# A transformer block on one core: side products in pairs of 64-row tiles between longer bursts of scores

## The reference

```python
h = _layernorm(x) * (1 + ca) + sa
qkv = (h @ qkv_w.T).reshape(B, S, 3, H, hd)             # B=4, S=1024, H=16, hd=16
scores = einsum('bhqd,bhkd->bhqk', q, k) * scale
out = einsum('bhqk,bhkd->bhqd', softmax(scores), v)
x = x + ga * (out.reshape(B, S, D) @ proj_w.T + proj_b)
h = _layernorm(x) * (1 + cb) + sb
base = h @ W_base + b_base
hid = relu(einsum('btd,ndh->nbth', h, W_enc) + b_enc)   # 8 experts of 64
recon = einsum('nbth,nhd->nbtd', hid, W_dec) + b_dec
adp = connected_idx[argmin(mean((recon - h) ** 2))]     # one per batch
mid = relu(h @ W_down[adp] + b_down[adp])
x = x + gb * (base + mid @ W_up[adp] + b_up[adp])
```

## Time and profile before

| | |
|---|---|
| median of 3 runs | 971.86 us (970.64 to 972.51) |
| the profiled execution, its own time | 975.65 us |
| its span in the trace | 973.8 us |
| PE busy | 938.1 us (96% of the span), 5890 matmuls |
| PEld (weight loads) busy | 489.1 us (50%) |
| DVE busy | 792.8 us (81%) |
| ACT busy | 656.7 us (67%) |
| POOL busy | 373.6 us (38%) |
| chain that ended last, share of PE | 76% |

### The profile page before, as it was taken

How to read it: one execution, slowest core, us unless ns; L and a number is a source line. 1 busy time by engine, 2 the same in 40 slices (tenths; PEclk the granted TensorE clock), 3 DMA queues, 4 the chain that set the end, 5 groups by cost and what they waited for, 6 DMA issues and landing times.

```text
span 973.8 us, 16714 instructions
## 1 busy us (share of the span) xinstructions
PE 938.1 (96%) x5890; PEld 489.1 (50%) x5890; DVE 792.8 (81%) x1629; ACT 656.7 (67%) x1295; POOL 373.6 (38%) x497
## 2 busy tenths in 40 slices
PE   6899999999999999999999999999999899999997
PEld 4443344434444555555444555645445465644486
DVE  4799989999788888877897888876887778888365
ACT  2148888888588677666679677575777756667930
POOL 4050265225366354121746645121655312115320
PEclk9889999999899999999999999999999999999999
DMA  7832061253444210555150511526123500141101
GB/s 179 142 73 45 23 115 58 60 122 82 70 75 77 59 45 25 83 82 168 48 86 20 94 57 35 83 54 170 52 64 53 77 8 29 41 129 59 30 6 50
DMA packets 51427, 68.78 MB, mean 71 GB/s; under 512 B 12347, under 2 KB 35648, under 8 KB 51332
## 3 DMA queue, kind: packets, MB, share of 16 engines
q1 hardware_dynamic: 50108, 66.84, 32.1%
q0 software_dynamic: 384, 0.79, 0.6%
q10 hardware_dynamic: 852, 0.09, 0.1%
HBM read 29.31 MB, written 12.59 MB: 43 GB/s over the span
## 4 chain that ended last, share of the span: by engine, by line
PE 76%; DVE 10%; ACT 4%; DMA 3%; SPq 2%; issue 2%; POOL 1%; ACTq 0%; DVEq 0%
PE pE L849 26%; PE pM L849 21%; PE pO L849 20%; PE pX L849 7%; DVE mx L1344 6%; DMA QO<-lo 2%; ACT P L1170 2%; SPq L1949 1%; DMA xin<-in_x 1%; DVE junk L1538 1%; ACT h2l_full L1257 1%; SPq L2009 1%; DMA P<-in_wmod 0%; DVE junk L1481 0%; ACT h1l_full L1211 0%
## 5 line engine op out<-in xcount | busy, mean ns | idle before, releaser
L1344 DVE TENSOR_REDUCE mx<-pM 128x1 f32<-128x512 f32 x458 | 298.6, 682 | 43.7 <-PE pM L849 41.6
L1170 ACT ACTIVATE P<-pM 128x512 f32<-128x512 f32 x464 | 260.2, 602 | 70.7 <-PE pM L849 69.4
L1344 DVE TENSOR_REDUCE mx<-pE 128x1 f32<-128x512 f32 x428 | 284.2, 681 | 28.9 <-PE pE L849 27.8
L1170 ACT ACTIVATE P<-pE 128x512 f32<-128x512 f32 x413 | 240.5, 602 | 83.4 <-PE pE L849 82.7
L849 PE MATMUL pO<-P,V 128*17 128x512 f32 x2048 | 261.0, 604 | 0.3 <-ACT P L1170 0.2
L849 PE MATMUL pM<-KO,QO 48*128 48x512 f32 x458 | 182.7, 456 | 8.2 <-DMA QO<-lo 6.5
L849 PE MATMUL pE<-KO,QO 48*128 48x512 f32 x428 | 179.0, 445 | 2.1 <-DVE mx L1344 1.3
L849 PE MATMUL pM<-QO,KO 50*128 50x512 f32 x464 | 174.1, 435 | 0.9 <-DVE mx L1344 0.5
L849 PE MATMUL pE<-QO,KO 50*128 50x512 f32 x413 | 170.7, 440 | 1.5 <-DVE mx L1344 1.0
L849 PEld LDWEIGHTS pM<-QO,KO 50*128 50x128 f32 x464 | 80.6, 188 | 85.0 <-issue 58.3
L849 PEld LDWEIGHTS pE<-QO,KO 50*128 50x128 f32 x413 | 73.8, 187 | 98.0 <-issue 76.5
(11 more groups left out here) (351 smaller groups left out, 1395.8 us busy)
## 6 DMA issues: line engine op xcount, KB each, us to landing
outs<-osb SPq DMA_DIRECT2D x31, 256.0 KB, 2.1
KO<-hi SPq DMA_DIRECT2D x56, 128.0 KB, 4.0
QO<-hi SPq DMA_DIRECT2D x56, 128.0 KB, 5.8
x<-in_x SPq DMA_DIRECT2D x20, 256.0 KB, 3.4
out<-x SPq DMA_DIRECT2D x16, 256.0 KB, 2.1
AT<-outs SPq DMA_DIRECT2D x15, 256.0 KB
asum<-wsum SPq DMA_DIRECT2D x15, 256.0 KB
KO<-lo SPq DMA_DIRECT2D x28, 128.0 KB, 4.1
```

The lines of the kernel that those rows point to most:

```text
L1170: e.activation(P[:, u % 3, j, :], bank(s), ACT.Exp).then_inc(*empties(s))
L1344: e.tensor_reduce(mx[:, hq % 2, k:k + 1, kh], bank(s), AX.X, ALU.max, negate=True).then_inc(*empties(s))
```

## The change

The side steps of `mate` (`qk` and `v` of batches 1 to 3, `enc`, `half`, `gsq`, `base`, `out`, `proj`, apart from most of those behind the last E) come in pairs of two neighbouring steps. Each product is cut along its contraction in rows 0 to 63 and rows 64 to 127. The first step takes the lower rows while the second takes the upper ones, then they swap (`together`), so that a pair stands in the same 64-row form as the scores. A pair is cut in six chunks, three before and three after the swap; the fourth waits for the last matmul of the third (`s_swap`). In the main loop a pair gets a mixed burst of eight pairs of scores, with a chunk behind the second to the seventh (`MIXED`); both steps' banks stay held over it. A burst without a side pair is still of three. `long` is gone; pieces that don't pair are placed singly. The planner's lags and due times change with it. In the hand-written end, `gsq` of the last half moves ahead of the second pieces of three `half` steps, and DVE splits `wdn` into `wdh` and `wdl` one step earlier, with `mid` waiting for `wdl` only ahead of its third matmul.

```diff
-SHARE = (1.3, 1.8, 2.2, 2.4)
+SHARE = (1.0, 1.0, 0.8, 0.8)
+CAP = 3
+MIXED = (0, 1, 1, 1, 1, 1, 1, 0)
+def mate(s):
+    i = 2 if s[0] in ("half", "gsq", "v", "enc", "base", "proj", "out") else 3
+    if s[0] not in ("half", "gsq", "v", "enc", "base", "proj", "out", "qk") or s[i] % 2:
+        return None
+    if s[0] in ("qk", "v") and s[1] == 0 or s[0] in ("proj", "out") and s[1] == LAST and (s[0] == "out" or s[2] > 1):
+        return None
+    return s[:i] + (s[i] + 1,) + s[i + 1:]
...
-        for _ in range(BURST):
+        credit = min(credit + SHARE[min(int(u) // UB, LAST)], CAP)
+        both = next_of("pair", u) if credit >= 1 and m < NM - 9 and at + len(MIXED) <= 4 * pv + 12 else None
+        credit -= both is not None
+        parts_done = 0
+        for i in range(1, (len(MIXED) if both else BURST) + 1):
...
+            for _ in range(MIXED[i - 1] if both else 0):
+                chunk(both, u, parts_done)
+                parts_done += 1
...
+            def products(s, h):
+                kind, b, k = s[:3]
+                o, r = bank(s), slice(64 * h, 64 * h + 64)
...
+                    if kind == "out":
+                        m0, r_ = 128 * (tt % 4), slice(64, 65) if h else slice(0, 64)
+                        got.append((region, hidden_of(b, k // 2)[r_, m0:m0 + 128], wug[r_, :]))
+                return got
+            def together(first, second, q):
+                if q == 0:
+                    inputs(first)
+                    inputs(second)
+                p, i = divmod(q, 3)
+                if q == 3:
+                    pe.wait_ge(*swap.now())
+                both = list(zip(products(first, p), products(second, 1 - p)))
+                n = len(both)
+                for k in range(n * i // 3, n * (i + 1) // 3):
+                    x, y = both[k]
+                    a = mm(*x, start=p == 0 and k == 0, stop=p == 1 and k == n - 1)
+                    z = mm(*y, start=p == 0 and k == 0, stop=p == 1 and k == n - 1)
+                if q == 2:
+                    z.then_inc(*swap.up())
...
-    for i in range(2):
-        for p in range(3):
-            fill(first[1][p], i)
-    now(("gsq", q, 0, 1), ("gsq", q, 1, 1), first[1][3], ("pick", q))
+    for p in range(3):
+        fill(first[1][p], 0)
+    now(("gsq", q, 0, 1), ("gsq", q, 1, 1))
+    for p in range(3):
+        fill(first[1][p], 1)
+    now(first[1][3], ("pick", q))
...
-                elif s == ("mid", LAST, 0) and not piece:
+                elif s == ("base", LAST, 3) and not piece:
```

More of the change, by code:

```diff
@@ L272, in come, with can, chunk @@
         for s in due.get(u, ()):
-            queue = waiting["short" if s[0] in SHORT else "quiet" if s[0] in QUIET else "long"]
+            if s in seconds:
+                continue
+            seconds.add(mate(s))
+            queue = waiting["short" if s[0] in SHORT else "quiet" if s[0] in QUIET else "pair" if mate(s) else "long"]
             queue.insert(sum(w[0] == "qk" for w in queue) if s[0] == "qk" else len(queue), s)
+    def can(s, u):
+        return all(done.get(p, u + 1) + lag <= u for p, lag in before(s) + (before(mate(s)) if mate(s) else []))
+    def chunk(s, u, q):
+        out.extend([(s, q // 5), (mate(s), q // 5, s)] if q in (0, 5) else [("chunk", s, mate(s), q)])
+        if q == 5:
+            done[s] = done[mate(s)] = u
+            if s[0] == "qk":
+                moving.extend(copies(4 * s[1] + s[2]))
     def next_of(queue, u, two=False):
@@ L284, in next_of @@
                 continue
-            if all(done.get(p, u + 1) + lag <= u for p, lag in before(s)):
+            if can(s, u):
                 waiting[queue].remove(s)
-                return (s, 0) if s[0] in PIECES else s
+                return (s, 0) if s[0] in PIECES and queue != "pair" else s
         return None
-    def ready(u):
-        return len(begun) + sum(all(done.get(p, u + 1) + lag <= u for p, lag in before(s)) for s in waiting["long"])
     def put(s, u):
         out.append(s)
-        step, p = s if isinstance(s[0], tuple) else (s, 0)
+        step, p = s[:2] if isinstance(s[0], tuple) else (s, 0)
         if p + 1 < PIECES.get(step[0], 1):
@@ L345, in alone_long @@
                 put(s, u)
+                if begun:
+                    put(begun.pop(), u)
     def alone(u0):
         for i in range(2):
-            out.extend(("E", u0 + i, j) for j in range(4))
+            both = next_of("pair", u0 + i)
+            for j in range(4):
+                out.append(("E", u0 + i, j))
+                if both and j % 2:
+                    for q in range(3 * (j // 2), 3 * (j // 2) + 3):
+                        chunk(both, u0 + i, q)
             if i == 0:
@@ L375, in weigh, with beside @@
             waiting["quiet"][:0] = [("oput", hq)] + [(k, *part) for k in ("oget", "orec", "osum", "onorm") if last]
-    credit, at, pv = 0.0, 0, 0
+    def beside(u):
+        held = any(s[0] in ("orec", "osum", "onorm") and (s[2:] == (1, 1) or ("oget", *s[1:]) in done)
+                   for s in waiting["quiet"])
+        for _ in range(6 if moving and moving[0][1] == 4 * NB - 1 else 3):
+            if moving and not (URGENT and any(x[0] == "mturn" for x in waiting["short"])) and (
+                    moving[0][1] < 4 or done["qk", *divmod(moving[0][1], 4), 1] + SPLITS <= u) and (not held or u > 8 * SEQ.index((moving[0][1], 0)) - LEAD // 4 - 6) and (moving[0][1] < 3 or at >= 32 * (SEQ.index((moving[0][1] - 3, 1)) + 1)):
+                out.append(moving.popleft())
+                if not moving or moving[0][1] != out[-1][1]:
+                    done["moved", out[-1][1]] = u
+        s = next_of("quiet", u)
+        if s:
+            put(s, u)
+    credit, at, pv, bare = 0.0, 0, 0, False
     while at < 4 * NU:
@@ L419, in order @@
                 pv += 1
-            filled = 0
-            if n == 1 and not light:
-                credit, filled = long(u, min(credit + 1, 2))
-        else:
-            stood = len(out)
-            credit, filled = long(u, min(credit + SHARE[min(int(u) // UB, LAST)], 2 if light else 3.5), 2 - light)
-            if len(out) == stood and some:
-                weigh(pv, u)
-                pv += 1
-        for _ in range(2 - (filled > 1)):
+        for _ in range(0 if both else 2):
+            if n or begun:
+                s = next_of("long", u)
+                if s:
+                    put(s, u)
+        for _ in range(2 if n or bare else 0):
             s = next_of("short", u)
@@ L435, in order @@
                     break
+        bare = not n
         s = next_of("quiet", u)
@@ L858, in tensor @@
                     o = bank(s)
-                if kind == "E":
+                if s in S.mates:
+                    if S.nth[s] > S.nth[S.mates[s]]:
+                        together(S.mates[s], s, 5 * piece)
+                elif kind == "chunk":
+                    together(*s[1:])
+                elif kind == "E":
                     u, j = s[1:]
@@ L1518, in vector @@
                     dve.wait_ge(*emptied(*s))
-                elif kind == "gsq":
+                elif kind == "gsq" and last:
                     b, i, th = s[1:]
```

189 lines of the change are left out of this document (121 added, 68 removed).

## The result

The changed kernel takes 1000.83 us in the median of 4 runs (1000.61 to 1005.73), the kernel before 971.25 beside it (970.24 to 972.51): ratio 1.031, interval 1.0287 to 1.0333. I had forecast 937. The profiled execution took 1000.61 us, its span is 998.8 and the mean granted clock 0.967, against 975.65, 973.8 and 0.981 before.

The account below looks back on a forecast made before the run. PE, always busy, was taken to lose 0.20 us per stretch of one form (ACT bounds E alone). Fewer stretches -42.4, waits +7.8 and the end -0.4 sum to -35.0 on 975.65: 940.6, or 937 us against 971.86; range 912 to 966.

Parts of the forecast that it names:

- two signs that I had named for a wrong prediction: In the profile after: chunks running slower than 0.117, or six-pair bursts, priced from only 11, costing more.
- Fewer stretches: On PE, 719 stretches of one form become 507; 212 fewer at 0.20 us each give -42.4 us.
- One-row products: In six `out` pairs, 24 products over row 64 make 48 stretches at 0.20; if free, 9.6 us more won.
- A mixed burst's wait: In 61 mixed bursts: 0.184 of a three-pair burst plus 0.1 for the swap, 0.284 us each, 17.3 in all.
- The rival of a slow VectorE: DVE without reserve makes each mixed burst wait 0.7 us, 25 us more: 962 us; chance 0.20.
- The bound of 1.16: Upper end of a mixed burst's wait, a six-pair burst's price; as the bank rival 990 us, chance 0.06.
- the 0.86 at which I had the sign turn: Wait per mixed burst, 0.284 + 35/61 us, from which the slower-by-banks rival is decided.
- Plain bursts: Waits of 85 three-pair bursts at 0.184 and 37 six-pair at 1.16 us, against 68.0 for all bursts before.
- Weight loads: In side pairs both halves' loads overlap as the scores' do: 0; one at a time +69 us, 1006 us, chance 0.05.
- Planner and queues: 0: Operands of a head group still copied well ahead, SP and POOL far from their bounds: 0.
- The end: After the last E: `mid` waits only for `wdh`, not the last addition, and `wdl`'s wait falls away: -0.4 us.
- By quarter: By stage: first -8.6 for stretches and +10 for waits, then -10.5, -12 and -14 us; E alone 0.

Follow-up runs that it names:

- full_height: The changed kernel in its own order of steps, but each half chunk written as a full-height one, without swap or one-row products: 1094.58 us, ratio 1.1272.
- pad_row: The changed kernel with the one-row part of each `out` pair given 64 rows, 63 of them zeros: 975.59 us, ratio 1.0011.
- singles: The changed kernel without pairs: the new planner's numbers and rules kept, every side step alone at full height: 1030.5 us, ratio 1.0587.

## Why the prediction was wrong

In the ledger's terms I had forecast -35 and measured +26. Of these 61 us the mixed and `out` bursts make 42, the clock 15, the work 6.5 (5.1 of it the one-row products') and the rest 2; the stretches, of which more went than I had priced, give 5 back. The steps that failed are 2, 3, 6 and 7 below. Neither of the two signs that I had named for a wrong prediction showed: the chunks run at 0.117, and a six-pair burst costs 1.08 us and not more than 1.16.

1. **Fewer stretches, -42.4: right in kind.** The 0.20 is confirmed by `full_height`. Counted with the one-row products apart, 235 stretches are gone, -47.0; my count of 212 plus 48 one-row ones made it 52.0.
2. **One-row products, 0.20 for each of 48 changes, 9.6 in all: the failed step that cost most for its size.** They are a form of their own, as I said, but I priced only the change. Their own work comes on top, since nothing runs beside them: +5.1 of work and +12.5 of waits in six bursts, and the clock falls with them. `pad_row` puts it at 25 us. The Trainium skill, "TensorEngine Tiling (Array Packing)", Key Properties, states the drain at a change of mode. The trace agrees as far as it shows: from 445.26 to 446.11 nothing starts in either half but the one-row product and its mate.
3. **A mixed burst's wait, 0.284: the failed step with the largest sum.** It is 0.71 us in 59 bursts (42.1 us) and 2.85 in the six `out` bursts (17.1): 59.2 against 17.3. Without the one-row part 48.2 remain, 31 more than forecast. The rival of a slow VectorE had the size (0.7 a burst) but named the wrong engine, so its size is luck. I compared 0.69 us a pair of PE with 0.682 of DVE and left out that ScalarE, too, returns one bank for each pair, and that a late half is not made good inside the burst. Of the 0.74 us in `pad_row` the runs show at least 0.30 for the two readers and 0.12 for the exchange; 0.32 stays open. The bound of 1.16 was not reached by the 59. Over all 65 bursts the mean is 0.91, just above the 0.86 at which I had the sign turn.
4. **Plain bursts: right.** 85 x 0.184 + 37 x 1.16 - 68.0 = -9.5 against -10.1 in the ledger. But the six-pair bursts are part of the change, not of its surroundings: -38.5 on three-pair bursts is given back to three quarters by 26 more of six.
5. **Weight loads 0: right.** Both halves load together, 0.117 and 0.231 hold.
6. **"Planner and queues: 0": failed.** I looked only at how far ahead the copies are. The new due times put `sbc` beside `addx`. In E alone I had the change at nothing, since ACT bounds it, and there the kernel loses 15.9 us, more than anywhere else. In `pad_row`, without the one-row part, 9.2 of them stay: PE has side products of 10.7 us of distances there (parts of `enc`, `proj` and `out`) where before had 4.2 (`enc`), and ScalarE, which bounded the stage, waits for PE for over 10 us instead of 3. `singles` loses 6.3 us in this stage without any pair.
7. **The clock: missing from the sum.** +15.0 in the ledger, of which `pad_row` keeps 3.3. The mean granted clocks say the same: (1 - 0.967) x 998.8 - (1 - 0.981) x 973.8 = 14.5 us.
8. **The end, -0.4: right**, -0.6 in the change and -0.3 alone.

By quarter the forecast was 0 to -3, -10.5, -12 and -14. In `pad_row`, without the one-row part, the middle three give -6.8, -6.4 and -8.0, some 60% of it. The first quarter, at +13.4, takes most of this away, about 10 us of it by the clock (27 us at the lower level against 7), and E alone another 9.2. In `singles` the first quarter is 11.6 us longer than before, so most of this loss isn't the pairs'. (DVE's share in the fourth quarter before was 81%, not 82 to 83; nothing hangs on it.)

## What to carry to other kernels

When two products are packed side by side, price the burst by every engine that frees a bank in it, and price what can't be packed with the rest (another tile height) at its full length and not at the cost of the change. Before making stretches longer, look what the longest one in the old trace costs: here three pairs were about what the banks hold, six cost 1.1 us more, and the planner made such bursts wherever a burst had no side work behind it. Test a new order without the new feature, too: here it was 58 us slower by itself. A forecast that counts on an always busy PE needs a term for the clock as well: here waits of 2.1 and 3.0 us were followed by 10 and 7 us at the lower level.

## What was unexpected of the hardware

- A product over one row with 128 columns stopped the other row half: 24 of them cost 25 us with their waits, and with 63 rows of zeros added they cost nothing to be seen.
- In a packed burst one late half stayed late: after a score product held for a bank, the halves ran 0.08 us apart or more until they next waited for each other.
- The `sbc` products took 0.82 us on VectorE beside POOL's additions and 0.42 without.
